# Keys and values of the first two context batches made in the last part of the memory attention, and twenty instead of ten slot clearings queued first

## What is computed

```python
# phase 0: a memory of two matrices and a scale, trained on the tokens in four chunks, then asked with queries
mem_f, _ = jax.lax.scan(step, (mem0, surp0), xs)            # four steps, each with its gradients
x = x + mem_fwd(mem_f, rmsnorm(silu(xn @ wq.T)))
# phase 1: 8 heads of 32; keys and values come from the context (8, 256, 512), a given input
k, v = split(ctx @ W_src + b_src); q = xn @ W_tgt + b_tgt     # q and k times the mask rows
attn = softmax(where(mask == 0, -inf, q k^T / sqrt(32)))
x = x + concat([xn, attn @ v]) @ W_out.T + b_out
```

## Time and profile before

| | us |
|---|---|
| median of three timed runs | 2446.67 (2442.28 to 2450.27) |
| the profiled execution | 2438.51 |
| its span, first to last instruction | 2436.7 |
| phase 0 ends | 418.95 |
| phase 1, start to end | 419.06 to 654 |
| TensorE busy, whole span | 2027.6 (83%) |
| DVE / ACT / POOL busy | 1469.2 / 1094.9 / 749.3 |
| mean granted clock of TensorE | 0.917 of full (2.4 GHz; the other level is 1.2 GHz) |

### The profile page before, as it was taken

The page is one execution under the profiler, slowest core; times in us unless marked ns, Lnnn a source line. Parts: engine busy times, 40 slices in busy tenths (PEclk is TensorE's granted clock), DMA queues, the critical chain, the costliest instruction groups (busy, mean ns, idle before and its releaser), DMA issues.

```text
span 2436.7 us, 35005 instructions
## 1 busy us (share of the span) xinstructions
PE 2027.6 (83%) x12078; PEld 1385.1 (57%) x12078; DVE 1469.2 (60%) x4614; ACT 1094.9 (45%) x2670; POOL 749.3 (31%) x752
## 2 busy tenths in 40 slices
PE   4888878989799998887768999668687898999779
PEld 3544445767546554455544778557555456666546
DVE  5655535544465557787641676498677855666662
ACT  2233332544352332376620365677566323666332
POOL 3122124121132231234432355355343331011353
PEclk9899988998799999899879999878899898999889
DMA  6804992100100002101134255400230000000000
GB/s 247 297 0 165 325 334 83 56 27 1 57 1 1 1 1 85 36 19 34 48 132 141 88 146 155 158 1 1 72 116 15 28 1 16 1 1 2 37 1 35
DMA packets 40302, 180.38 MB, mean 74 GB/s; under 512 B 6816, under 2 KB 24352, under 8 KB 36992
## 3 DMA queue, kind: packets, MB, share of 16 engines
q1 hardware_dynamic: 32496, 157.04, 19.0%
q0 software_dynamic: 7632, 21.11, 2.5%
HBM read 154.93 MB, written 98.89 MB: 104 GB/s over the span
## 4 chain that ended last, share of the span: by engine, by line
PE 62%; DVE 17%; ACT 11%; POOL 4%; issue 4%; DMA 0%; another core or an unknown queue 0%; POOLq 0%; DVEq 0%; SPq 0%; ACTq 0%
PE ps L216 40%; PE ps L739 5%; ACT BIG L816 4%; PE ps L711 3%; PE ps L758 3%; PE ps L1908 3%; PE ps L281 2%; ACT BIG L291 1%; PE ps L1920 1%; DVE BIG L291 1%; DVE XN L272 1%; DVE BIG L779 1%; PE ps L845 1%; PE ps L1312 1%; DVE SML L257 1%
## 5 line engine op out<-in xcount | busy, mean ns | idle before, releaser
L216 PE MATMUL ps<-BIG 128*128 128x256 f16 (+2 forms) x1616 | 340.7, 360 | 26.0 <-DVE BIG L2509 12.9
L816 ACT ACTIVATE BIG<-BIG,SML 128x256 f32<-128x256 f32 (+1 forms) x768 | 302.5, 482 | 17.4 <-DVE SML L779 17.1
L216 PEld LDWEIGHTS ps<-BIG 128*128 128x128 f16 (+1 forms) x1616 | 223.3, 140 | 120.7 <-issue 65.7
L739 PE MATMUL ps<-CST,BIG 128*128 128x128 f32 x1408 | 222.9, 295 | 55.0 <-ACT BIG L816 39.4
L739 PEld LDWEIGHTS ps<-CST,BIG 128*128 128x128 f32 x1408 | 165.6, 149 | 134.1 <-ACT BIG L816 86.8
L636 POOL TENSOR_TENSOR BIG<-BIG 128x512 f16<-128x512 f32 x120 | 142.3, 1187 | 293.5 <-ACT BIG L570 265.3
L216 PE MATMUL ps<-XN,BIG 128*128 128x512 f16 x864 | 205.1, 393 | 14.2 <-ACT BIG L547 5.3
L291 ACT ACTIVATE BIG<-ps 128x512 f32<-128x512 f32 (+1 forms) x240 | 127.2, 563 | 176.7 <-PE ps L739 112.6
L779 DVE CUSTOM_DVE_ANT_0 BIG<-ps,BIG 128x256 f32<-128x256 f32 x512 | 181.2, 420 | 37.3 <-PE ps L711 28.0
L220 POOL TENSOR_SCALAR SML<-SML 128x4 f32<-128x4 f32 (+1 forms) x88 | 24.5, 278 | 505.7 <-DVE SML L260 245.4
L291 DVE COPY BIG<-ps 128x512 f32<-128x512 f32 (+1 forms) x176 | 110.3, 638 | 104.3 <-PE ps L739 89.8
(11 more groups left out here) (401 smaller groups left out, 3965.5 us busy)
## 6 DMA issues: line engine op xcount, KB each, us to landing
slots<-in_zeros SPq DMA_DIRECT2D x28, 2640.0 KB, 65.4
WA<-slots SPq DMA_DIRECT2D x95, 132.0 KB
BIG<-in_l1e SPq DMA_DIRECT2D x2, 4224.0 KB
BIG<-spread SPq DMA_DIRECT2D x16, 512.0 KB, 5.2
BIG<-in_l0e SPq DMA_DIRECT2D x8, 768.0 KB, 7.9
BIG<-in_ctxT SPq DMA_DIRECT2D x8, 512.0 KB, 4.0
BIG<-in_ctxT SPq DMA_DIRECT2D x16, 256.0 KB, 3.0
BIG<-in_ctx SPq DMA_DIRECT2D x16, 256.0 KB, 3.3
```

The source lines that it names most:

```text
L216: m = T.e.matmul(ps, l, r, start=i == 0, stop=i == len(pairs) - 1)
L739: m = T.e.transpose(PS[r][:, o:o + P], c["SM"][n % 2 * 4 + i][:, q, tok(k)], ident)
L816: A.e.activation(s[:, q, 0:kn[q]], s[:, q, 0:kn[q]], ACT.Exp, bias=mx[:, q:q + 1], scale=-1.0).then_inc(*(A.sig("exp", p, n, i) if q else ...
```

## The change

Four pieces of work move from phase 1 into the last part of phase 0: the keys and values of batches 0 and 1 (`early_1_pe`, `early_1_dve`). Each is a group of 16 matmuls of 256 columns in bank 5 with two DVE evictions behind it. The keys of batch 0 follow the fourth memory step, its values follow the first hidden layer, the keys of batch 1 follow the output of group 1 and its `norm_turn`, its values the output of group 3. GpSimd writes the zero and one columns after the memory's last update and masks the values of batch 0 in group 0; those of batch 1 it masks at the start of phase 1. The buffers of phase 1 get other places in `SCR`, so that each lies where phase 0 is done. `load_1` now comes in two parts: contexts once the gradient g1 of the last step is made, mask row and column once g0 is. Twenty clearings instead of ten go ahead of the weights, eight behind them. From batch 2 on nothing changes in what is computed or in the order.

```diff
         def shared_1():
-            get = scratch((0, 7680), (11776, SCRN))
-            c = attend(1, 8, [range(0, 4), range(4, 8)], [2 * P, 2 * P], get, spare_wa0(), "AAAA")
-            c["QB"], c["KB"] = ([get(512).rearrange("p (k s) -> p k s", k=2) for _ in range(2)] for _ in range(2))
+            c = attend(1, 8, [range(0, 4), range(4, 8)], [2 * P, 2 * P], scratch((0, 3072), (5632, 6656)), spare_wa0(),
+                       "AAAA", scratch((3328, 5376)))
+            get = scratch((11776, 12800), (13824, 14848))
+            c["KB"], c["QB"] = ([get(512).rearrange("p (k s) -> p k s", k=2) for _ in range(2)] for _ in range(2))
...
-            for name, pairs in (("qp", lambda m: [(wtgt[:, i, tok(m)], XT[:, i, b * 256:(b + 1) * 256]) for i in range(2)]),
-                                ("kp", lambda m: [(wsrc[:, i, tok(m)], ct[:, i, :]) for i in range(4)]),
-                                ("vp", lambda m: [(ct[:, i, tok(m)], wsrc[:, i, 256:512]) for i in range(4)])):
+            for name in ("qp",) if made_1(b) else ("qp", "kp", "vp"):
                 for m in range(2):
                     r, before = c["RT"].take((name, b, m), (name + "c", b, m))
                     waits(T, *before)
-                    group(PS[r][:, 0:256], pairs(m)).then_inc(*T.sig(name, b, m))
+                    group(PS[r][:, 0:256], [(wtgt[:, i, tok(m)], XT[:, i, b * 256:(b + 1) * 256]) for i in range(2)]
+                          if name == "qp" else pairs_1(c, b, name, m)).then_inc(*T.sig(name, b, m))
                     yield
+
+        def made_1(b):
+
+            return b < 2 and begun(1)
+
+        def pairs_1(c, b, name, m):
+            wsrc, ct = W[1]["wsrc"].rearrange("p (k n) -> p k n", k=4), c["CT"][b % 2]
+            if name == "kp":
+                return [(wsrc[:, i, tok(m)], ct[:, i, :]) for i in range(4)]
+            return [(ct[:, i, tok(m)], wsrc[:, i, 256:512]) for i in range(4)]
+
+        def early_1_pe(c, ring, b, name):
+
+            r, before = ring.take((name, b), (name + "c", b, 0), (name + "c", b, 1))
+            waits(T, *before)
+            waits(T, ("w1",), (f"ctx{b}", b))
+            for m in range(2):
+                t = group(PS[r][:, m * 256:(m + 1) * 256], pairs_1(c, b, name, m))
+            t.then_inc(*T.sig(name, b, 1))
+
+        def early_1_dve(c, b, name):
+            waits(V, ("mrow",), (name, b, 1))
+            if name == "vp":
+                waits(V, ("ones", 1, b))
+            for m in range(2):
+                src = bank(name, b)[:, m * 256:(m + 1) * 256]
+                if name == "kp":
+                    V.e.scalar_tensor_tensor(c["KB"][b][:, m, :], src, W[1]["bk"][:, m:m + 1],
+                                             c["mrow"][:, b * 256:(b + 1) * 256], ALU.add, ALU.mult).then_inc(
+                        *V.sig("kpc", b, m))
+                else:
+                    V.e.tensor_tensor(c["VA"][b][:, m, :].rearrange("p (h w) -> p h w", w=c["w"])[:, :, 0:c["dh"]],
+                                      src.rearrange("p (h d) -> p h d", d=c["dh"]),
+                                      W[1]["bv"].rearrange("p (h d) -> p h d", d=c["dh"]), ALU.add).then_inc(
+                        *V.sig("vpc", b, m))
+
...
-            for name, dst, bias in (("qp", c["QB"], "bt"), ("kp", c["KB"], "bk")):
+            for name, dst, bias in (("qp", c["QB"], "bt"), ("kp", c["KB"], "bk"))[:1 if made_1(b) else 2]:
...
-            yield from values_in(c, b, "vp", w["bv"], "vpc")
+            if not made_1(b):
+                yield from values_in(c, b, "vp", w["bv"], "vpc")
...
         def l0_xattn_pool(c):
-            ones_columns(c)
+            if begun(1):
+                masked_values_1(c, 1)
+            else:
+                ones_columns(c)
             add_bias(1, W[1]["bo"], range(NG - 1))
-            waits(G, ("mcol",))
             for b in range(B + 4):
...
         def load_1(c):
+            if begun(1):
+                waits(SP, ("g1", 3, 1))
+            for b in range(2):
+                SP.e.dma_start(c["CT"][b], a["ctxT"][:, b, :, :]).then_inc(*SP.sig(f"ctx{b}", b, by=16))
+            if begun(1):
+                waits(SP, ("g0", 3, 1))
             SP.e.dma_start(c["mrow"], a["fk1_row"]).then_inc(*SP.sig("mrow", by=16))
             SP.e.dma_start(c["mcol"], a["fk1_col"]).then_inc(*SP.sig("mcol", by=16))
-            for b in range(2):
-                SP.e.dma_start(c["CT"][b], a["ctxT"][:, b, :, :]).then_inc(*SP.sig(f"ctx{b}", b, by=16))
...
-            return p in (4, 7) and p - 1 in phases
+            return p in (1, 4, 7) and p - 1 in phases
...
-                clear_slots(0, 200)
+                clear_slots(0, 400)
             if after(0) is not None:
                 waits(SP, ("kv", 15))
                 weights(after(0))
             if 5 in phases:
-                clear_slots(200, SLOTS)
+                clear_slots(400, SLOTS)
             if after(0) == 1:
-                waits(SP, ("w0", 3), ("w1", 3), ("ln", 3), ("g5", 3))
                 load_1(S1)
...
             for n in range(4):
                 chunk_pe(c, n, fill)
+            if after(0) == 1:
+                early_1_pe(S1, c["RF"], 0, "kp")
             waits(T, ("w1", 3), ("w0", 3))
...
             hidden(0)
+            if after(0) == 1:
+                early_1_pe(S1, c["RF"], 0, "vp")
             waits(T, ("normc", 3))
...
                     t.then_inc(*T.sig("qy", g, jj))
+                if after(0) == 1 and g == NG - 1:
+                    early_1_pe(S1, c["RF"], 1, "vp")
                 if g and after(0) is not None:
                     norm_turn(c["RQ"], after(0), g - 1)
+                if after(0) == 1 and g == 1:
+                    early_1_pe(S1, c["RF"], 1, "kp")
             if after(0) is not None and not ends_later(after(0), NG - 1):
...
             for n in range(4):
                 chunk_dve(c, n, fill)
+            if after(0) == 1:
+                early_1_dve(S1, 0, "kp")
...
             hidden(0)
+            if after(0) == 1:
+                early_1_dve(S1, 0, "vp")
             for g in range(NG):
...
                 if g and after(0) is not None:
                     norm_copy(V, after(0), g - 1, 1)
+                if after(0) == 1 and g == 1:
+                    early_1_dve(S1, 1, "kp")
                 if after(0) is not None and not ends_later(after(0), g):
...
             if after(0) is not None and not ends_later(after(0), NG - 1):
                 norm_copy(V, after(0), NG - 1, 1)
+            if after(0) == 1:
+                early_1_dve(S1, 1, "vp")
...
             for n in range(4):
                 chunk_pool(c, n, fill)
+            if after(0) == 1:
+                waits(G, ("ln", 3))
+                ones_columns(S1)
             lay(fill, 2)
...
                 if g + 1 < NG:
                     finish(asked[g + 1])
+                if after(0) == 1 and g == 0:
+                    masked_values_1(S1, 0)
                 if g + 2 < NG:
...
```

More of the change, by code:

```diff
@@ L956, in prep_1_pe @@
         def prep_1_pe(c, b):
-            wsrc, wtgt = W[1]["wsrc"].rearrange("p (k n) -> p k n", k=4), part("wtgt", 1)
-            ct = c["CT"][b % 2]
+            wtgt = part("wtgt", 1)
             waits(T, ("w1",), (f"ctx{b % 2}", b))
-            for name, pairs in (("qp", lambda m: [(wtgt[:, i, tok(m)], XT[:, i, b * 256:(b + 1) * 256]) for i in range(2)]),
-                                ("kp", lambda m: [(wsrc[:, i, tok(m)], ct[:, i, :]) for i in range(4)]),
-                                ("vp", lambda m: [(ct[:, i, tok(m)], wsrc[:, i, 256:512]) for i in range(4)])):
+            for name in ("qp",) if made_1(b) else ("qp", "kp", "vp"):
                 for m in range(2):
@@ L969, in prep_1_dve, with masked_values_1 @@
+        def masked_values_1(c, b):
+            waits(G, ("mcol",))
+            for k in range(2):
+                waits(G, ("vpc", b, k))
+                v = c["VA"][b % 2][:, k, :].rearrange("p (h w) -> p h w", w=c["w"])[:, :, 0:c["dh"]]
+                G.e.tensor_scalar(v, v, c["mcol"][:, 2 * b + k:2 * b + k + 1], None, ALU.mult).then_inc(
+                    *(G.sig("vm", b) if k else G.step()))
         def prep_1_dve(c, b):
@@ L1137, in l0_xattn_pool @@
         def l0_xattn_pool(c):
-            ones_columns(c)
+            if begun(1):
+                masked_values_1(c, 1)
+            else:
+                ones_columns(c)
             add_bias(1, W[1]["bo"], range(NG - 1))
-            waits(G, ("mcol",))
             for b in range(B + 4):
[L1142 to L1147, removed]
+                if b < B and not made_1(b):
+                    masked_values_1(c, b)
                 if b == 1 and ends_later(1, NG - 1):
```

## The result

| | before | after |
|---|---|---|
| median of four timed runs each, us | 2447.77 (2442.28 to 2450.27) | 2429.62 (2426.87 to 2434.22) |
| profiled execution; span, us | 2438.51; 2436.7 | 2426.87; 2425.1 |
| mean granted clock of TensorE | 0.917 | 0.923 |
| mean granted clock, about 300 to 419 us | 0.89 | 0.97 |

The ratio is 0.9931, with a 95% interval of 0.9905 to 0.9956: 17 us faster. Two later series put the ratio lower: 0.990 [0.9885, 0.9915] on the same chip, and 0.9907 [0.9893, 0.992] on a second one, where the kernel before took 2412.57. The three estimates of the gain lie between 17 and 25 us.

The account below looks back on a forecast made before the run. TensorE was taken to bound phase 1 and to wait in late phase 0. 10.5 + 0.5 − 0.3 + 1.9 − 0.8 = 11.8 us off the 2446.67 median gave 2434.9, range 2427 to 2443.

Parts of the forecast that it names:

- rival (b): The clock gains more: high through rounds 0 to 2 and in phase 0's late part, 17.0 us, 2429.7; chance 0.18.
- the second turn: Late phase 0: 2.4 us gained where this turn starts at the low clock, counted only in rival (b).
- Part 1: Front of phase 1: keys and values of batch 0 leave, so the first maximum comes 6.8 us earlier.
- Part 2: Phase 1, rounds 0 and 1: keys and values of batch 1 leave; gain 3.7 us, taken at the low clock.
- Nothing is given back from round 2 on: Phase 1 from round 2: TensorE has as much to do as before and stays the bound, so the gain holds.
- Parts 3 to 6: Late phase 0, the four moved groups: 0.5 gained, 0.3 lost, 1.9 gained, 0.8 us lost.
- The second hole's delay: Late phase 0, values of batch 0: two DVE evictions delay the scaling of the next queries, cost 0.3 us.
- The third turn: Late phase 0, keys of batch 1: 2.0 us gained by the clock on 48 matmuls, less 0.1, so 1.9.
- Part 7: DMA queue: twenty clearings first let contexts and mask row land in time; the shift itself costs nothing.
- Rival (c): Loads come late at the end of phase 0: DVE carries 46 us, 34 us slower, 2481; chance 0.04.
- (a): Low clock past round 3 and in phase 0's holes eats the gain: 4.3 us in all, 2442.4; chance 0.15.
- (d): Something other than the moved matmuls holds round 0, such as ScalarE's first exponential: 5 us, 2442; chance 0.05.

Follow-up runs that it names:

- the repeat: The changed kernel timed once more with nothing else changed, against the kernel before: 2423.62 against 2447.54, ratio 0.990.
- the other trace of the old order on this chip: The kernel before with twenty clearings ahead of the weights and eight behind, nothing else: 2443.01, ratio 0.9989.
- warm starts: The changed kernel with six spare products at the end of phase 0: 2427.33, 0.993; with the early function table load too, on the second chip: 2384.04, 0.9889.

## Why the forecast was right in kind and short in size

The time lies in the range, faster as forecast, and that it lies there is in part luck: the first series gave the smallest of the three gains, and the repeat, 2423.62, is past the fast end of 2427. The mechanism was right: the matmuls left a stretch where TensorE was the bound and went to where it waited. But 11.8 us was too little, and rival (b), 17.0 us and 2429.7, came nearest. Its number is partly chance as well: the 2.4 us that it had for the second turn did not come (the second hidden layer took 9.74 us before and 9.73 after), and 3.2 us came at the end of phase 1, which it didn't have. By the steps of the forecast:

- **Part 1, right.** VectorE's first maximum, beside the earlier trace rows, is at 425.88, 6.60 us after the start instead of 13.12: 6.5 us for 6.8. The difference is the mask, which took 0.70 us and not 0.3.
- **Part 2, mis-sized; this is the step that failed.** From the first maximum to the scores of round 2 it is 9.7 us instead of 15.7. I had 10.0 at the high clock, 11.9 at the low one, and chose the low one since TensorE's work gets sparse there. The granted clock was low only at the start of that stretch, so the gain was 6.0 us, not 3.7:

```profile
426.00:429.00 3.00, 3.00 (x8) 2.15 (x8) 3.00 (x17) 2.23 (x4) 2.83 (x3) 0.58 1.02 426
429.00:432.00 3.00, 2.86 (x30) 2.04 (x29) 0.89 (x3) 3.00 (x8) 0.53 (x1) 1.00 1.01 416
```

It stayed at 1.00 up to 435. The row did not carry over; why the clock rose here and not there, no run shows. With part of the stretch low, 9.7 us is also less than the 10.0 for the high clock, so the hand-overs had been put too long by a little.
- **"Nothing is given back from round 2 on", wrong twice.** Round 3 gave back 1.5 us: the scores of round 2 fell to the low clock (2.09 us now, 1.15 in the earlier trace rows). And rounds 11 to 15 gained 3.2 us. Phase 1 as a whole: 6.5 + 6.0 − 1.5 + 3.2 = 14.2 us against 10.5, and phase 1 was 221.1 to 221.3 us long in all five traces that start it as after does.
- **Parts 3 to 6, the signs right, the sum too low.** The piece from the memory update to the first hidden layer gained 1.05 (0.5 forecast). The granted clock in the hole, 0.63 in 312.60 to 317.20 by the earlier trace rows, is 1.00 in the same piece of after, 315.85 to 320.45. That it fell 1.2 us after TensorE stopped holds for that one trace: with the clearings alone moved, the mean in the same empty hole (316.1 to 320.8) is 0.87, so it fell later, and it was then low, 0.50 to 0.52, up to 330. The second hole's delay was 0.46 (0.3), but the warmer queries behind it brought 0.55 that I had left at nothing. The third turn brought 2.2 + 0.4 (1.9), the end cost 0.7 (0.8): 3.0 us in this pair against 1.3, up to 5.2 against the other trace of the old order on this chip, the one with the slow first hidden layer.
- **Part 7, right.** The mask row landed at 316.4, wanted at 320.9. That the clearings cost the engines nothing agrees with their own experiment.
- **Rival (c), the right price by two errors.** Forecast 34 us slower, measured 36.8. The wait was 61 us and not 46: the contexts came at 376.7, right behind the last clearing (149.1 us after its issue at 226.3, so at 375.4), where I had taken the mask row's landing of the earlier trace rows, 364, though the last clearing of the same group landed at 371. And the gain on the other side was 24 us, not 11.8.
- **Rivals (a) and (d)** are out: the low clock took back no more than 1.5 us of phase 1's gain, phase 0 gained where (a) had it lose 2.7, and ScalarE's exponential, though on the chain, holds round 0 no longer than forecast.
- **The reference point.** The profiled run of before was 8.2 us below the median of its three runs, that of after only 2.8 below its own, so the profiles differ by less (11.6 us) than the timed runs do.
- **The chances.** Their summary is off by 0.01: (a) and (d) make 0.20, not 0.19, and the slower cases 0.07.

Open: on the first chip the two stretches behind phase 2 take 63.5 and 289 to 290.5 us in every trace with batch 0 moved (but for the one with ten clearings first, 64.6 and 296.8) and 64.2 and 292.5 to 293.5 in those without; nothing was changed there, and I don't know the cause. With them the stretches give 14.3 + 3.0 to 5.2 + some 3.5 = 21 to 23 us, which fits the timed 17 to 25; without them, since they were not touched, 17 to 20. Nor do I know why the low clock behind the wait ahead of round 14 ends early in one order and late in the other. Whether warm starts, which shorten phase 1 by 3 us in the trace, shorten the kernel, these runs are too few to tell.

## What to carry to other kernels

Dense matmuls taken from a loop that TensorE bounds and put into short waits elsewhere pay twice, by their length and by keeping the clock up where they land: look for both, and try spare products alone to learn what the second is worth. A filler must stand exactly in its wait: eight products one wait late took 3.7 us of a TensorE that was busy. Compare two traces stretch by stretch at fixed marks, since stretches that were not touched can differ by 3 us and hide or mimic the effect. Before a load is moved earlier, work out what stands in its queue: here the same load took 4.8 or 69.7 us by that alone.

## What was not expected of the hardware

- Filling four waits of TensorE with products that nobody uses made the kernel 8.6 us faster (0.9961 [0.9947, 0.9975]).
- Behind one and the same 4.0 us wait the granted clock stayed low for over 9 us in one order and some 3 us in the other: from round 14 to 15 it is 8.4 us in four profiles, 5.9 in six, 6.9 in two.
- In the same hole of 4.75 us, with the same work in front of it, the mean granted clock was 0.63 in one trace and 0.87 in another. Where it fell later it also came back later, and the first hidden layer behind it took 8.37 instead of 7.03 us.
- Stretches of equal code come out in two lengths about 3.2 us apart (196.3 to 196.6 and 199.4 to 199.9, with one at 197.5; 403.9 to 404.0 and 407.1 to 407.4) from kernel to kernel.
